# Causal attention with a gated channel mix on one core: scores kept transposed in an SBUF ring, the last query block of each batch in two groups

## The reference

```
n1 = layernorm(x)
q = (n1 @ Wq + bq) / 16;  k = n1 @ Wk + bk;  v = n1 @ Wv + bv
scores = q @ k.T, causal;  ctx = softmax(scores) @ v
x1 = x + ctx @ Wo + bo
n2 = layernorm(x1);  prev = n2 shifted down by one row
r = sigmoid((mu_r*n2 + (1-mu_r)*prev) @ W_r)
k = (mu_k*n2 + (1-mu_k)*prev) @ W_k
out = x1 + r * (square(relu(k)) @ W_v)
```

## Time and profile before

| | |
|---|---|
| median of 3 runs | 406.23 us (404.18 to 407.58) |
| the profiled execution, first to last instruction | 404.5 us |
| TensorE busy | 381.2 us, 2607 matmuls |
| VectorE busy | 306.3 us |
| ScalarE busy | 226.2 us |
| GpSimd busy | 141.3 us |
| DMA | 10.81 MB, 27 GB/s on average |

### The profile page before, as it was taken

The page is one execution under the profiler, slowest core; times in us unless marked ns, Lnnn a source line. Parts: engine busy times, 40 slices in busy tenths (PEclk is TensorE's granted clock), DMA queues, the critical chain, the costliest instruction groups (busy, mean ns, idle before and its releaser), DMA issues.

```text
span 404.5 us, 7159 instructions
## 1 busy us (share of the span) xinstructions
PE 381.2 (94%) x2607; PEld 345.6 (85%) x2607; DVE 306.3 (76%) x808; ACT 226.2 (56%) x514; POOL 141.3 (35%) x186
## 2 busy tenths in 40 slices
PE   5879999899999999999989989999999889999966
PEld 4768998799989999899978979889998779898946
DVE  1688977997879966766899946987669966954763
ACT  2345467557575455762656666547448367556543
POOL 2053420542553241425322562535122520731630
PEclk9999999999999999999999999999999999999976
DMA  7700000000300002003000000020010000000100
GB/s 176 226 2 1 2 2 0 3 0 2 104 2 1 2 28 78 2 0 105 1 2 0 2 2 23 4 78 2 0 53 2 1 0 2 23 31 2 52 24 30
DMA packets 12034, 10.81 MB, mean 27 GB/s; under 512 B 1888, under 2 KB 12000, under 8 KB 12000
## 3 DMA queue, kind: packets, MB, share of 16 engines
q1 hardware_dynamic: 12000, 10.36, 8.5%
HBM read 6.17 MB, written 4.19 MB: 26 GB/s over the span
## 4 chain that ended last, share of the span: by engine, by line
PE 67%; DVE 24%; issue 4%; ACT 2%; DMA 1%; POOL 1%; SPq 0%; DVEq 0%
PE G L732 7%; PE G L736 7%; PE G L735 7%; PE S L735 6%; PE PT L861 6%; PE S L732 6%; PE S L736 6%; PE O L732 6%; PE O L736 6%; PE O L735 6%; DVE mix L646 4%; PE G L766 3%; DVE x_in L599 2%; DVE pT_lo L477 2%; DVE scratch L524 2%
## 5 line engine op out<-in xcount | busy, mean ns | idle before, releaser
L329 ACT ACTIVATE pT_hi<-PT 128x512 fp32r<-128x512 f32 (+2 forms) x80 | 42.5, 532 | 98.6 <-PE PT L861 98.5
L732 PE MATMUL O<-v_hi,pT_hi 128*128 128x256 f32 x272 | 79.5, 292 | 0.0
L736 PE MATMUL O<-v_hi,pT_lo 128*128 128x256 f32 x272 | 76.8, 283 | 0.0
L735 PE MATMUL O<-v_lo,pT_hi 128*128 128x256 f32 x272 | 76.7, 282 | 0.0
L373 ACT ACTIVATE prob<-prob,neg_max 128x512 f32<-128x512 f32 (+2 forms) x80 | 52.1, 651 | 18.5 <-DVE neg_max L578 18.5
L735 PE MATMUL S<-kT_lo,xT_hi 128*128 128x512 f32 (+2 forms) x160 | 61.3, 383 | 0.0
L732 PE MATMUL S<-kT_hi,xT_hi 128*128 128x512 f32 (+2 forms) x160 | 58.8, 368 | 0.0
L736 PE MATMUL S<-kT_hi,xT_lo 128*128 128x512 f32 (+2 forms) x160 | 58.3, 364 | 0.0
L288 POOL TENSOR_TENSOR mix_lo<-mix,mix_hi 128x512 fp32r<-128x512 f32 (+1 forms) x32 | 41.4, 1314 | 41.6 <-ACT mix_hi L329 41.6
L265 POOL TENSOR_SCALAR var_eps<-mean_var 128x1 f32<-128x1 f32 (+1 forms) x40 | 8.9, 224 | 134.3 <-DVE mean_var L626 97.1
L477 DVE TENSOR_TENSOR pT_lo<-PT,pT_hi 128x512 fp32r<-128x512 f32 (+2 forms) x80 | 47.8, 597 | 9.7 <-ACT pT_hi L329 9.6
(11 more groups left out here) (136 smaller groups left out, 953.4 us busy)
## 6 DMA issues: line engine op xcount, KB each, us to landing
x_in<-in_L_attn_y_all_dram SPq DMA_DIRECT2D x8, 512.0 KB, 5.0
out_dram<-gate SPq DMA_DIRECT2D x15, 256.0 KB, 2.1
h_row<-in_L_attn_Wk_dram SPq DMA_DIRECT2D x1, 256.0 KB, 2.8
h_row<-in_L_attn_Wq_dram SPq DMA_DIRECT2D x1, 256.0 KB, 3.0
o_sum<-in_L_attn_Wv_dram SPq DMA_DIRECT2D x1, 256.0 KB, 6.1
o_sum<-in_L_attn_Wo_dram SPq DMA_DIRECT2D x1, 256.0 KB, 6.3
mix<-in_L_ffn_W_k_dram SPq DMA_DIRECT2D x1, 256.0 KB, 4.2
mix<-in_L_ffn_W_r_dram SPq DMA_DIRECT2D x1, 256.0 KB, 4.5
```

What stands on the lines that cost most here:

```text
L329: a.activation(dst, src, ACT.Copy, **kw).then_inc(done, 1)
L732: mm(dst, a_hi, b_hi, start=n == 0, stop=False)
L735: mm(dst, a_hi, b_lo, start=False, stop=False)
L736: last = mm(dst, a_lo, b_hi, start=False, stop=end)
```

## The change

Keys and queries change places in the scores: a step (`STEPS`, now `(J, j)`) is one tile of 128 keys against all queries of a group J, so the bank S holds transposed scores. A group is a block of 512 queries; each batch's last block makes two groups of 256. That is 10 groups and 108 steps.

ScalarE moves each step's scores, with e as a bias for each partition, to a place in an SBUF ring `st` of 16 tiles (`keep_scores`). VectorE keeps the elementwise maximum over a group's steps in `peak` (`take_max`). When the group is through, `gather_peak` transposes it, `peak_part` reduces it to one number per query, `spread_peak` and ScalarE make a tile `peak_b` of it. Then for each step, at a slot that is a table's: VectorE subtracts (`shift`), ScalarE takes the exponential and the high part (`exps`), GpSimd the low part (`weights_low`), TensorE multiplies by v (`pv`), accumulating a query tile's whole sum in one of four banks O. The row sum comes from a column of ones in `v_hi` (`VW = 258`). The scaling of o_sum, alpha, the row sums and the transposes of the probabilities are gone; banks PT are too.

x comes from HBM twice: `x_raw` (one buffer) for the first norm, `x_in` (now three) for the residual. `act_hi`, `act_lo` share memory with `mix_hi`, `mix_lo`. The slot tables are new; the slots go to 366, of which those from 108 on hold only products and stages.

The core of the diff:

```diff
-    NX = 4
+    NX = 3
     NT = 2
+    VW = C + 2
+    NR = 16
+    NP = 3
...
-    STEPS = [(G, c, p) for G in range(NG - 1) for c in range(G % GB + 1) for p in range(TG)]
-    STEPS += [(NG - 1, c, p) for p0 in range(0, TG, 2) for c in range(GB) for p in (p0, p0 + 1)]
+    GROUPS = []
+    for G in range(NG):
+        GROUPS += [(G, 0, TG)] if G % GB < GB - 1 else [(G, 0, TG // 2), (G, TG // 2, TG // 2)]
+    NJ = len(GROUPS)
+    LAST = NJ - 1
+    COUNT = [TG * (G % GB) + t0 + n for G, t0, n in GROUPS]
+    FIRST = [sum(COUNT[:J]) for J in range(NJ + 1)]
+    STEPS = [(J, j) for J in range(NJ) for j in range(COUNT[J])]
...
+        J, j = STEPS[s]
+        return j - TG * (GROUPS[J][0] % GB)
+    def tiles_of(s):
+        G, t0, n = GROUPS[STEPS[s][0]]
+        return range(max(t0, diagonal(s)), t0 + n)
+    def cols_of(s):
+        t0 = GROUPS[STEPS[s][0]][1]
+        q = tiles_of(s)
+        return slice((q.start - t0) * P, (q.stop - t0) * P)
...
+            if size == TG and d == TG - 1:
+                found.append((found[s - 2][0], 0))
+            elif size == TG // 2 and j % 2:
+                found.append((found[s - 1][0], GW // 2 + cols_of(s).start))
+            else:
+                found.append((n, cols_of(s).start))
+                n += 1
...
+    MT_AT = [(4,), (13,), (24,), (38,), (54,), (58,), (67,), (78,), (92,), (127,)]
+    MB_AT = [(4,), (15,), (26,), (41,), (54,), (59,), (68,), (80,), (95,), (128,)]
...
+    P_AT = [max(PV_AT[u - NP] + 1 if u >= NP else 0, MB_AT[STEPS[u][0]][0] + 1) for u in range(NS)]
+    P_IN = {s: [u for u in range(NS) if P_AT[u] == s] for s in SLOTS}
...
+            def load_raw(G):
+                if G > 0:
+                    sp.wait_ge(xhat_ready, TG * G)
+                sp.dma_start(x_raw[:], y_t[:, G * TG:(G + 1) * TG, :]).then_inc(raw_loaded, 16)
...
+            load_raw(1)
+            for G in range(NX):
                 load(G)
+            load_raw(2)
...
+                if G + 3 < NG:
+                    load_raw(G + 3)
...
+            def weights_low(u):
+                r = cols_of(u)
+                pool.wait_ge(p_high, u + 1)
+                g.tensor_tensor(p_lo[:, u % NP, r], score_tile(u), p_hi[:, u % NP, r].bitcast(f32), ALU.subtract)\
+                    .then_inc(p_split, 1)
...
+            def keep_scores(s):
+                J, j = STEPS[s]
+                tile = (GROUPS[J][0] // GB) * GB * TG + j
+                n = PLACES[s][0]
+                sc.wait_ge(s_ready, s + 1)
+                if diagonal(s) >= 0:
+                    sc.wait_ge(dotted, tile + 1)
+                if n >= NR:
+                    sc.wait_ge(p_split, FILLED[n - NR] + 1)
+                a.activation(score_tile(s), bank_s[s % 2][:, cols_of(s)], ACT.Identity, bias=e_col[:, tile:tile + 1])\
+                    .then_inc(st_ready, 1)
...
+            def exps(u):
+                sc.wait_ge(sub_done, u + 1)
+                a.activation(score_tile(u), score_tile(u), ACT.Exp).then_inc(exp_done, 1)
+                sc.wait_ge(exp_done, u + 1)
+                if u >= NP:
+                    sc.wait_ge(pv_done, u - NP + 1)
+                high(p_hi[:, u % NP, cols_of(u)], score_tile(u), p_high)
...
+                v.bn_stats(stats[:, t, :], x_raw[:, t, :]).then_inc(stat1, 1)
...
-                v.tensor_tensor_reduce(out=prob[:, s % 2, 0:w], in0=bank_s[s % 2][:, 0:w], in1=e_row[:, c * GW:c * GW + w],
-                                       scale=1.0, scalar=before, op0=ALU.add, op1=ALU.min,
-                                       accum_out=neg_max[:, c % 2, p:p + 1]).then_inc(s_used, 1)
...
-                low(pT_lo[:, s % 2, 0:w], bank_p[s % 2][:, 0:w], pT_hi[:, s % 2, 0:w], pT_split)
...
+            def take_max(s):
+                J, j = STEPS[s]
+                r = cols_of(s)
+                dve.wait_ge(st_ready, s + 1)
+                if j == 0:
+                    if J > 0:
+                        dve.wait_ge(mt_ready, J)
+                    v.tensor_copy(peak[:, r], score_tile(s)).then_inc(maxed, 1)
+                else:
+                    dve.wait_ge(maxed, s)
+                    v.tensor_tensor(peak[:, r], peak[:, r], score_tile(s), ALU.max).then_inc(maxed, 1)
...
+                v.tensor_reduce(peak_col[:, J % 2, 0:n], bank_of("mt", J, 0)[:, 0:n * P].rearrange("p (t k) -> p t k", k=P),
+                                axis=AX.X, op=ALU.max).then_inc(peak_ready, 1)
...
+            def shift(u):
+                J = STEPS[u][0]
+                if u == FIRST[J]:
+                    dve.wait_ge(mb_done, J + 1)
+                v.tensor_tensor(score_tile(u), score_tile(u), peak_b[:, cols_of(u)], ALU.subtract).then_inc(sub_done, 1)
...
+                v.reciprocal(inv_sum[:, p:p + 1], o[:, C:C + 1]).then_inc(inv_ready, 1)
...
+                v.scalar_tensor_tensor(x1, o[:, 0:C], inv_sum[:, p:p + 1], x1, ALU.mult, ALU.add).then_inc(o_used, 1)
...
+                if diagonal(s) >= t0:
+                    mask = (bank[:, r.start:r.start + P], ident_b[:], mask_b[:])
+                product(bank[:, left:r.stop],
+                        [(kT_hi[:, k, keys], kT_lo[:, k, keys], xT_hi[:, G % NT, k, q], xT_lo[:, G % NT, k, q])
...
-            def pT(s):
-                pe.wait_ge(exp_done, s + 1)
-                for b in range(width(s) // P):
-                    last = nc.tensor.transpose(bank_p[s % 2][:, b * P:(b + 1) * P], prob[:, s % 2, b * P:(b + 1) * P], ident[:])
-                last.then_inc(pT_ready, 1)
...
+            def gather_peak(J):
+                n = GROUPS[J][2]
+                free("mt", J, 0)
+                pe.wait_ge(maxed, FIRST[J + 1])
+                bank = bank_of("mt", J, 0)
+                for t in range(n):
+                    last = nc.tensor.transpose(bank[:, t * P:(t + 1) * P], peak[:, t * P:(t + 1) * P], ident[:])
+                last.then_inc(mt_ready, 1)
+            def spread_peak(J):
+                n = GROUPS[J][2]
+                free("mb", J, 0)
+                pe.wait_ge(peak_ready, J + 1)
+                bank = bank_of("mb", J, 0)
+                for t in range(n):
+                    last = nc.tensor.transpose(bank[:, t * P:(t + 1) * P], peak_col[:, J % 2, t:t + 1].to_broadcast([P, P]), ident[:])
+                last.then_inc(mb_ready, 1)
...
+            def pv(u):
+                J, j = STEPS[u]
+                G, t0, n = GROUPS[J]
+                c0 = cols_of(u).start
+                pe.wait_ge(p_split, u + 1)
+                if diagonal(u) == 0:
                     pe.wait_ge(v_split, 2 * (G + 1))
-                product(bank_o[s % 2][:, 0:C],
-                        [(pT_hi[:, s % 2, b * P:(b + 1) * P], pT_lo[:, s % 2, b * P:(b + 1) * P],
-                          v_hi[:, c * TG + b, :], v_lo[:, c * TG + b, :]) for b in range(width(s) // P)])\
-                    .then_inc(o_ready, 1)
-            pe.wait_ge(const_ready, 7)
+                for i, q in enumerate(tiles_of(u)):
+                    if j == 0 and G > 0 and i == 0:
+                        pe.wait_ge(o_used, TG * (G - 1) + t0 + n)
+                    w = slice(c0 + i * P, c0 + (i + 1) * P)
+                    end = diagonal(u) == q
+                    mm(bank_o[q][:, 0:VW], p_hi[:, u % NP, w], v_hi[:, j, :], start=j == 0, stop=False)
+                    mm(bank_o[q][:, 0:C], p_hi[:, u % NP, w], v_lo[:, j, :], start=False, stop=False)
+                    last = mm(bank_o[q][:, 0:VW], p_lo[:, u % NP, w], v_hi[:, j, :], start=False, stop=end)
+                last.then_inc(pv_done, 1)
...
-                if s + 2 < NS:
-                    scores(s + 2)
-                if s == -1:
+                if s in (0, 4):
+                    pe.wait_ge(ffn_split, 2 if s == 0 else 3)
+                if s == 0:
                     pe.wait_ge(bias_ready, 1)
-                if 0 <= s + 1 < NS:
-                    pT(s + 1)
...
+                if 0 <= s < NS:
+                    scores(s)
...
+                for u in PV_IN[s]:
+                    pv(u)
...
```

More of the change, by code:

```diff
@@ L131, in attention_channel_mix_block @@
         kT_hi, kT_lo = sb("kT_hi", [P, KC, T], f32r), sb("kT_lo", [P, KC, T], f32r)
[L132 to L135 removed]
+        v_hi, v_lo = sb("v_hi", [P, T // P, VW], f32r), sb("v_lo", [P, T // P, C], f32r)
+        st = sb("st", [P, NR, GW])
+        p_hi, p_lo = sb("p_hi", [P, NP, GW], f32r), sb("p_lo", [P, NP, GW], f32r)
+        peak, peak_b = sb("peak", [P, GW]), sb("peak_b", [P, GW])
+        peak_col = sb("peak_col", [P, 2, TG])
         hT = sb("hT", [P, KC, GW + 1])
@@ L307, in _ @@
             for s in SLOTS:
-                if diagonal(s - 1):
-                    rsqrt2(STEPS[s - 1][0], STEPS[s - 1][2])
+                for u in P_IN[s]:
+                    weights_low(u)
+                for u in DONE_IN.get(s - 1, ()):
+                    rsqrt2(u)
                 for stage, n, i in STAGES.get(s - 1, ()):
@@ L315, in _ @@
                         rsqrt1(n)
```

(42 more changed lines are left out.)

393 lines of the change are left out of this document (171 added, 222 removed).

## The result

The changed kernel takes **446.88 us** (median of 4, 445.76 to 448.48) against 405.49 for the kernel before (404.18 to 407.58): a ratio of 1.1022, 95% interval 1.098 to 1.1065, **slower by 10%**. Forecast were 392 us and a range of 374 to 412. The profiled execution took 448.48 us with a span of 446.7.

A forecast was written before the change was run, and what follows sets the result against it. TensorE's matmul stream was taken to set the time: 404.5 us less 24.3 of its work, plus 6.5 beside a fuller VectorE and 4.5 at the end, gives 391.2; likeliest 392, range 374 to 412.

The forecast's parts named there:

- TensorE's work: Matmuls and transposes: 272 transposes fewer, less the added transposes, scores and columns, change TensorE's time by -24.3 us.
- Products of 258 columns: Probability times value: 544 products two columns wider cost +0.5 us, between nothing and 60.
- The helpers' loads: Busy times after the change: VectorE 339 us, ScalarE at most 308, GpSimd 237, later near 250.
- Raw loads: Second load of x: costed at nothing; if its cover failed, VectorE would stand up to 5 us, once or twice.
- +6.5: Stretches with VectorE nearly full: TensorE loses 7.6% in half its work, 12.5 us, of which about 6 exist already.
- the +4.5 at the end: After the last block's first step: GpSimd's work is 9 us longer than TensorE's, half hidden by the 16-tile ring.
- 65 us of VectorE time: VectorE held up by GpSimd in SBUF: 52 us on new instructions and 13 on those that stay.
- three passes: ScalarE per step: keep the score, exponential, high part; 172 us of busy time in all.
- C: Rival: GpSimd and VectorE exclude each other for each whole instruction, so their times add: 415 us, slower; chance 0.17.
- B: Rival: the queues absorb all delays, 382 us, down to 376 if the mid-kernel stalls vanish; chance 0.22.
- its own sign: The sign for B: the new maximum and shift on VectorE run at their free durations, 0.68 us at 512.
- D: Rival: the transposes' gain is given back in waits, last group's chain plus late raw load, near 406 us; chance 0.13.

The follow-up runs named there:

- e6: e1 with the running maximum taking only 8 columns of each step: 405.81 us.
- e1: The changed kernel, but GpSimd writes zeros as the low part of the probabilities, one write per step, instead of subtracting: 427.3 us.
- e2: The changed kernel, but GpSimd writes zeros as the low part of the probabilities in several small pieces instead of subtracting: 427.92 us.
- e10: The changed kernel, but ScalarE takes the exponential twice, into p_hi and in place, instead of exponential, wait, copy; nothing left out: 435.15 us.
- e9: e6 and e7 together, so low part, maximum and exponential are left out of the changed kernel: 393.24 us.
- e7: e1 with ScalarE's exponential and the wait for it left out, p_hi copied from the shifted score: 402.29 us.
- e15: e1 and e10 together on the changed kernel, low part left out: 415.53 us.
- e3: The changed kernel, same instructions, with new scores kept before exponentials not yet due, and the maximum before those steps' shifts: 474.57 us.
- e8: The changed kernel with the first batch's last block as one group of 512 queries, 94 steps, slot tables shifted untuned: 471.46 us.

## Why the prediction was wrong

**TensorE's work: right.** -24.3 was forecast, about -20 is what the split above leaves. Products of 258 columns are no dearer. The timeline of TensorE in the changed kernel (compare) has them 0.12 us apart:

```profile
164.73 0.28 PE L887 MATMUL O<-v_hi,p_lo 128*128 128x258 f32 x1
164.85 0.28 PE L885 MATMUL O<-v_hi,p_hi 128*128 128x258 f32 x1
164.97 0.28 PE L886 MATMUL O<-v_lo,p_hi 128*128 128x256 f32 x1
```

**The helpers' loads: right.** VectorE 339 forecast and 337.5 measured, GpSimd 250 and 249.2. ScalarE, at most 308, came to 270.0. Raw loads: x_raw is waited for once, for 7.2 us, at the start.

**The step that failed** is the one from these loads to TensorE's loss: "Of some 330 us of TensorE work I let half fall in such stretches: 165 x 0.076 = 12.5, of which about 6 are in today's span already", hence +6.5, and the +4.5 at the end. Its place is taken by 54.5 us more of waiting and 7.7 us at the half clock. I took the relation between a full VectorE and a waiting TensorE from one stretch of the kernel before and carried it to a kernel with another dependence, a chain over four engines. 7.6% was what TensorE lost beside an engine that is nearly full, and e6 shows another relation: there VectorE's 28 us are worth 21.5. What the runs put in its place:

- VectorE held up by GpSimd in the pass for the low part: 19 us (e1, e2 against the change). I had computed 65 us of VectorE time for it, and saw 28 go with e2 from this pass alone; wrong was that most of it would be hidden.
- ScalarE's exponential and the copy that waits for it: 12 us (e10), in the forecast nothing. I had priced three passes as busy time and set them aside as "not a bound on the whole".
- The maximum and the rest of the exponential pass on the path: with both taken out of e1 34 us (e9), of which the wait in e10 is a part, since e7 and e9 leave it out with the exponential.

These don't close the sum exactly: e15 is still 23 us above the 392 forecast, and no run took that apart further by itself. The split of the result section, made again over the experiments' traces (37 us of waiting before and 93 after by this second count), gives 71 in e2, 67 in e15 and 47 in e9. That makes it likely that the rest is the same kind of loss, helpers' time on the chain. Where in the order each microsecond is lost stays open, as does the cost of the split in two groups. The plainest rival left is the order itself: no run searched for better slot tables, and e3 shows that the order is worth tens of us.

**The clock.** After waits, TensorE's granted clock goes to 0.5 (1.2 GHz) for 3.4 to 6.8 us at a time, seven times between 72 and 437 us; the kernel before shows that only from 390 on (0.62 over its last stretch). There the same products are 0.21 apart:

```profile
94.94 0.41 PE L886 MATMUL O<-v_lo,p_hi 128*128 128x256 f32 x1
95.15 0.42 PE L887 MATMUL O<-v_hi,p_lo 128*128 128x258 f32 x1
95.36 0.42 PE L885 MATMUL O<-v_hi,p_hi 128*128 128x258 f32 x1
```

That dip began at 92.87, after TensorE had waited 2.5 us for a kept score, until 91.96. The others are alike: the first six began 0.2 to 1.8 us after the end of a wait of 2.1 to 4.6 us (three for a kept score, two for p_lo, one for kT_lo), the seventh after two waits of 1.2 and 1.4. So the dips come with the waits. The forecast had no term for them.

**The rivals.** C had the sign and the mechanism in kind: a VectorE instruction stands until the GpSimd instruction beside it has ended (64 of 67 above), and GpSimd's subtraction of 256 takes 0.87 us in the median beside a VectorE instruction with all its tensors in SBUF, against 0.735 alone. Its sum (413) was not the bound: the kernel takes 447, and without this exclusion in the low part (e2) still 428. That both engines are busy for 586.7 us together, in a span of 446.7, says nothing against it, since the waits count as busy. The rule of the Trainium skill, "SBUF — State Buffer", section "Who interferes with whom", says that a GpSimd instruction that only writes SBUF does not contend, and e2 bears that out: beside such a write a shift of 256 takes 0.414 us, alone 0.415. What the runs tie to this contention is 19 of the 41 us; GpSimd's other reads beside VectorE stay in e2, and no run takes them away. B (382) is refuted by its own sign, the means of the maximum and the shift: 0.87 and 0.88 at 512, as the forecast had them. D had the last group's chain as the place; a chain it was, but in every stretch of the kernel. A slower kernel had a chance of 0.17, and by another path. The profile of before could not show the chain, but it could be counted from the diff.

## What to carry to other kernels

Taking work off the fullest engine pays only if what feeds it doesn't get longer: count, for the changed kernel, the chain of engines from one product to the next with its waits, since here, with no helper above 76%, TensorE waited 54 us more, which no busy share announces. Keep the two-input work of VectorE and GpSimd apart, or give one of them an operand in PSUM, but look at how long that holds the bank. A wait of a helper is no loss as long as TensorE doesn't wait with it: look at the waits of the engine that should be the bound. When an order in in-order queues is written out by hand, two orders of the same work can be 28 us apart (e3), so a run that changes the work and the order together, as e8, doesn't price the edit.

## What was unexpected of the hardware

- It is not only the two-input forms of VectorE that stand. A tensor_scalar of 128x256 (h_row) has a mean of 740 ns: 0.41 in the median alone or beside small roots, 1.37 beside a long GpSimd instruction. A copy of 128x256 (peak) took 1.35. The statistics of the same x_in (128x256) don't stand: five of them fell beside a long GpSimd instruction and took 0.427 to 0.429, as all the others.
- GpSimd loses as well, if less: its addition for gate (128x512) went from a mean of 1305 to 1499 ns, up to 2.42 at 161.23.
- GpSimd's small roots and its writes of constants hold VectorE up by nothing that shows. Two normalisations at 153.13 took 0.73 together with a root beside them; the median of the 24 subtractions at 256 that fell beside nothing but a constant's write in e2 was 0.414 (worked out from the trace), against 0.415 with GpSimd idle.
